# Attention score stacks of 96 and 99 rows filled with zeros to 125 and 128

## The reference

```python
mod = (silu(c) @ wmod).reshape(8, 6, 1, -1)             # shift, scale, gate, for both parts
h = layernorm(x) * (1 + ca) + sa
q, k, v = split(einsum('bnd,ed->bne', h, w_in), 3)      # 16 heads of 16 channels
scores = einsum('bhqd,bhkd->bhqk', q, k) * 16 ** -0.5
scores = where(causal, -inf, scores)                    # keys after the query
attn = softmax(scores, axis=-1)
out = einsum('bhqk,bhkd->bhqd', attn, v)
x = x + ga * (einsum('bnd,ed->bne', out, w_out) + b_out)
```

## Time and profile before

| | us |
|---|---|
| three executions | 1735.08, 1741.03, 1741.37 |
| median | 1741.03 |
| the profiled execution, own time | 1726.74 |
| its span, first to last instruction | 1725.1 |

### The profile page before, as it was taken

One profiled execution on the slowest core, in us unless ns is written; L12 is line 12 of the kernel. 1 busy time (PEld: TensorE's weight loads), 2 busy tenths in 40 slices (PEclk: granted clock), 3 DMA queues, 4 the chain that ended last, 5 costly groups with the idle time before them and its releaser, 6 DMA issues.

```text
span 1725.1 us, 33029 instructions
## 1 busy us (share of the span) xinstructions
PE 1449.8 (84%) x10024; PEld 755.3 (44%) x10024; DVE 1180.8 (68%) x2306; ACT 911.7 (53%) x1795; POOL 734.0 (43%) x876
## 2 busy tenths in 40 slices
PE   3798998788998988989898888978889789889754
PEld 2353344344543444444453444434454344544343
DVE  4668676867677776777668675787757777677342
ACT  2056655655555555565545655555545655565612
POOL 2213314454353533555344543444445453344456
PEclk9789999999998999899998999999999999999968
DMA  3211122111311122111211113111122112211100
GB/s 104 55 63 49 48 78 74 57 39 56 100 64 35 52 69 88 56 53 51 96 51 49 46 57 101 55 38 50 57 91 69 41 44 68 70 57 49 50 33 25
DMA packets 101873, 102.98 MB, mean 60 GB/s; under 512 B 21296, under 2 KB 89912, under 8 KB 101696
## 3 DMA queue, kind: packets, MB, share of 16 engines
q1 hardware_dynamic: 98176, 91.59, 16.4%
q0 software_dynamic: 2560, 8.39, 1.3%
q10 hardware_dynamic: 960, 0.79, 0.2%
HBM read 31.74 MB, written 8.94 MB: 24 GB/s over the span
## 4 chain that ended last, share of the span: by engine, by line
PE 48%; DVE 21%; issue 12%; ACT 9%; POOL 5%; SPq 2%; DMA 2%; DVEq 1%; ACTq 0%; POOLq 0%
PE row_ps L1073 9%; PE val_ps L1097 9%; PE col_ps L1043 8%; PE dense_ps L1107 7%; DVE max_a L868 7%; PE dense_ps L1109 5%; PE dense_ps L1108 5%; ACT weights L712 4%; DVE mixed L981 3%; PE row_ps L1078 2%; DVE max_b L868 2%; PE dense_ps L1126 2%; DVE xn_c L907 1%; SPq L458 1%; DVE gated L965 1%
## 5 line engine op out<-in xcount | busy, mean ns | idle before, releaser
L712 ACT ACTIVATE weights<-col_ps 128x512 f32<-128x512 f32 (+1 forms) x1216 | 620.9, 580 | 473.0 <-PE col_ps L1043 470.9
L868 DVE TENSOR_REDUCE max_a<-row_ps 128x1 f32<-128x512 f32 (+3 forms) x864 | 550.3, 663 | 238.3 <-PE row_ps L1078 155.3
L1073 PE MATMUL row_ps<-k_stack,q_stack 96*128 96x512 bf16 (+3 forms) x1536 | 469.8, 344 | 51.6 <-DVE max_a L868 33.3
L1043 PE MATMUL col_ps<-q_stack,k_stack 99*128 99x512 bf16 (+3 forms) x1536 | 400.8, 337 | 54.0 <-ACT weights L712 33.8
L594 POOL TENSOR_SCALAR_AFFINE_SELECT weights<-weights 128x512 f32<-128x512 f32 x256 | 171.0, 668 | 543.2 <-ACT weights L712 541.1
L1097 PE MATMUL val_ps<-weights,v_ones 128*32 128x512 f32 (+3 forms) x3072 | 337.0, 511 | 16.7 <-POOL weights L594 16.1
L1073 PEld LDWEIGHTS row_ps<-k_stack,q_stack 96*128 96x128 bf16 x1536 | 146.7, 100 | 354.4 <-DVE max_a L868 168.1
L868 DVE TENSOR_REDUCE max_b<-row_ps 128x1 f32<-128x384 f32 (+3 forms) x352 | 213.2, 635 | 115.0 <-PE row_ps L1078 114.7
L1043 PEld LDWEIGHTS col_ps<-q_stack,k_stack 99*128 99x128 bf16 x1536 | 133.5, 99 | 221.3 <-ACT weights L712 138.3
L1078 PE MATMUL row_ps<-causal,ident_bf 128*128 128x128 bf16 x1024 | 207.4, 227 | 0.0
L1078 PEld LDWEIGHTS row_ps<-causal,ident_bf 128*128 128x128 bf16 x1024 | 104.4, 102 | 14.8 <-issue 0.5
(11 more groups left out here) (127 smaller groups left out, 2251.6 us busy)
## 6 DMA issues: line engine op xcount, KB each, us to landing
q_stack<-q_part SPq DMA_DIRECT2D x384, 64.0 KB, 2.5
k_stack<-k_part SPq DMA_DIRECT2D x372, 64.0 KB, 2.5
xa<-in_x SPq DMA_DIRECT2D x8, 1024.0 KB, 6.6
att<-val_out SPq DMA_DIRECT2D x64, 128.0 KB
recips<-recip_rows SPq DMA_DIRECT2D x32, 256.0 KB
xq<-in_x SPq DMA_DIRECT2D x28, 256.0 KB, 3.0
out<-xq POOLq DMA_DIRECT2D x28, 256.0 KB, 2.6
q_stack<-max_rows SPq DMA_DIRECT2D x192, 4.0 KB
```

What stands on the lines that cost most here:

```text
L712: nc.scalar.activation(weights[:, t % 2, h:h + n, 0:q1 - q0], col_ps[bank][:, 0:n * (q1 - q0)].rearrange("p (h q) -> p h q", h=n), ACT.Exp ...
L868: nc.vector.reduce_max(dest, bank[:, 0:len(heads) * (k1 - k0)].rearrange("p (h k) -> p h k", h=len(heads)), AX_X).then_inc(max_done, 1)
L1043: last = nc.tensor.matmul(col_ps[bank][:, i * (q1 - q0):(i + 1) * (q1 - q0)], k_stack[s % 2][:, h, P * j:P * (j + 1)], q_stack[s % 2][:, h ...
L1073: last = nc.tensor.matmul(bank[:, n * width:(n + 1) * width], q_stack[stack][0:ROWS, h, P * i:P * (i + 1)], k_stack[stack][0:ROWS, h, k0:k ...
```

## The change

The stacks get all 128 partitions. The maximum's three rows move from 96 to 98 to 125 to 127 (`MAX_AT`). Between them and the products' rows stand zeros in `q_stack`, written once in the set-up by two further GpSimd memsets, and ones in `k_stack`, whose memset now covers 32 rows. Row-score matmuls contract rows 0 to 124 instead of 0 to 95, column-score matmuls 128 rows instead of 99. The added rows add zero to each score. The number of instructions in the loop, their moving columns, the DMAs and their sizes, and all waits stay.

```diff
@@ -43,6 +43,7 @@
 ROWS = len(Q_PARTS) * HD
 MROWS = 3
+MAX_AT = P - MROWS
 FILL = 2 * len(Q_PARTS) * 16
@@ -146,8 +147,8 @@
-        q_stack = [sb(f"q_stack{i}", [ROWS + MROWS, G, N], BF16) for i in range(2)]
-        k_stack = [sb(f"k_stack{i}", [ROWS + MROWS, G, N], BF16) for i in range(2)]
+        q_stack = [sb(f"q_stack{i}", [P, G, N], BF16) for i in range(2)]
+        k_stack = [sb(f"k_stack{i}", [P, G, N], BF16) for i in range(2)]
@@ -530,7 +531,7 @@
                         for part in range(3):
-                            sp.dma_start(q_stack[s % 2][ROWS + part:ROWS + part + 1, :, HALF:N],
+                            sp.dma_start(q_stack[s % 2][MAX_AT + part:MAX_AT + part + 1, :, HALF:N],
                                          max_rows[1][G * part:G * part + G, :]).then_inc(max_placed[1], 16)
@@ -546,7 +547,7 @@
                         for part in range(3):
-                            sp.dma_start(q_stack[(s + 1) % 2][ROWS + part:ROWS + part + 1, :, 0:HALF],
+                            sp.dma_start(q_stack[(s + 1) % 2][MAX_AT + part:MAX_AT + part + 1, :, 0:HALF],
                                          max_rows[0][G * part:G * part + G, :]).then_inc(max_placed[0], 16)
@@ -564,6 +565,8 @@
             nc.gpsimd.memset(causal[:], 0.0)
+            for stack in q_stack:
+                nc.gpsimd.memset(stack[:], 0.0)
             nc.gpsimd.memset(neg_half[:], -0.5).then_inc(consts_zero, 1)
@@ -815,7 +818,7 @@
             for i in range(2):
-                nc.vector.memset(k_stack[i][ROWS:ROWS + MROWS, :, :], 1.0)
+                nc.vector.memset(k_stack[i][ROWS:P, :, :], 1.0)
@@ -1071,8 +1074,8 @@
                     last = nc.tensor.matmul(bank[:, n * width:(n + 1) * width],
-                                            q_stack[stack][0:ROWS, h, P * i:P * (i + 1)],
-                                            k_stack[stack][0:ROWS, h, k0:k1],
+                                            q_stack[stack][0:MAX_AT, h, P * i:P * (i + 1)],
+                                            k_stack[stack][0:MAX_AT, h, k0:k1],
                                             start=(n == 0), stop=(end and not diagonal), skip_group_check=True)
```

## The result

The change makes the kernel faster: 1717.7 us median of 9 runs (1711.6 to 1731.4) against 1741.4 us of the kernel before in the same set, ratio 0.987 with a 95% interval of 0.984 to 0.991. A second set gave 1721.6 against 1736.5 us, ratio 0.989 (0.986 to 0.993). The forecast was 1722 us.

A forecast was written before the change was run, and what follows sets the result against it. It took TensorE's pace, at a mean clock of 0.947, to bound a large part of the run. Terms 0 + 0 + 0 - 16 - 3 = -19 us gave 1708 us profiled, 1722 us against the median; range 1701 to 1741 us.

The forecast's parts named there:

- Height bears on the clock: TensorE's granted clock: contracted rows count toward it; the change raises height 30% in row scores, 29% in column scores.
- Durations, nothing: Score matmuls and weight loads: cost unchanged by height, 0 us, bounds -6 to +6 us.
- The rival of loads that no longer hide: Row scores: weight loads stop overlapping running matmuls; 1756 us if a tenth of each load surfaces; chance 0.08.
- Set-up, nothing: Set-up: two added GpSimd memsets, 7.0 us taken, fit in GpSimd's 22.87 us of idle time; 0 us.
- The clock in the middle, -16 us: Middle of the run: 53 of 107 us at low clock go, at 0.3 us each.
- The start, -3 us: Near the start: an earlier clock rise saves 1.3 us before 92.5 us and 1.7 us after; bounds 0 and 5.
- The tail, nothing: Tail from 1638 us on: no score matmul is left there, so 0 us.
- The sum: Whole kernel: all terms give -19 us against the profiled 1726.74 us, so 1708 us.
- The step to the median: Whole kernel: the -19 us applied to the timed median of 1741.03 us gives 1722 us, -1.1%.
- doesn't look at height: Rival, TensorE's clock: it ignores height, so the change does nothing and time is 1741 us; chance 0.12.
- Another engine takes the gain: Rival: the clock rises but another engine bounds; 53 us give 7, the start 1, so 1733 us; chance 0.13.
- More than forecast: Rival: TensorE bounds nearly everywhere, most low spells vanish; 80 us x 0.45 + 4 = 40 us, 1701 us; chance 0.15.

The follow-up runs named there:

- half the height: The change with the maximum's rows at 112 to 114, so row scores contract 112 and column scores 115 rows; 1725.7 us, 0.995 of the kernel before.
- the set-up alone: Kernel before plus 128-row stacks and their memsets only; scores stay at 96 and 99 rows, maximum's rows at 96; 1738.1 us, ratio 0.999.
- four fillers per unit: The change plus four matmuls with unread results behind each of the drain's 20 dense units; 1711.9 us, 0.987 of the kernel before.

## Why the prediction was right

*Height bears on the clock*: shown. With the loop's instructions, columns and waits unchanged, half the height gives about half the clock, all of it 0.022, the set-up alone nothing.

*Durations, nothing*: right. Row-score loads take 99 ns (100 before), 512-column matmuls 393 and 394 ns (401 and 399), which fits the higher clock. The rival of loads that no longer hide is out.

*Set-up, nothing*: right, 6.96 us of memsets against the 7.0 taken, in idle time, and 0.999 when alone.

*The clock in the middle, -16 us*: right in kind, and its size met with luck. The first pair of profiles differs by 16.5 us there, by terms that were off in opposite directions: 68 us of low clock went instead of 53, at 0.24 us each instead of 0.3. By the second set's profile 44 us of low clock and 7.0 us of length went. The kernel with the set-up alone, in which height is as before, had 134 us low and 1553.5 us; against it the two profiles of the change are 24.6 and 15.1 us shorter. The three spells of 13.6 us ended sooner, as forecast; the longest in the middle after the change is 6.8 us. What the s = 1 rows said (0.13) and what s = 0 said (0.36) were both samples around 0.25. Groups of s = 1 take 53.4 us in the loop on average (forecast 53 to 55), those of s = 0 55.7 (forecast 54 to 55, a miss: three of the five still have a spell).

*The start, -3 us*: 2.5 us for the same work, 36.8 instead of 39.3 us from the first row-score matmul to the 61st. The first column score comes 4.7 us sooner (84.2 instead of 88.9 us), but 4.0 of these were there at the first row score, ahead of any taller matmul. The prediction took the low clock near the start to begin at 61.8 us. It was low from 45 to 58.4 us too, as the 628 ns show, where the trace has no record of it, and when it first rises differs from profile to profile.

*The tail, nothing*: wrong of the two profiled executions, +9.1 us, most of it not the change's doing. Of the eleven profiled executions without fillers in the tail all but one have 62 to 80 us low in it and 89.5 to 91.9 us of length, the set-up alone too (66 and 89.8). The kernel before's profile is the one exception, with 37 and 82.8. What the change itself does there is less clear: the seven with column scores of 128 rows have 69 to 80 us low, the four with fewer rows 37 to 66. Why is open.

*The sum*: against the profiled execution it was to be 1708 and came to 1714.8: start, middle and tail made -4.7, -16.5 and +9.1 us, and 4.0 us of the first are not the height's. The second set's profile has 1725.0. Against the median, 1722 forecast and 1717.7 measured, and 1721.6 in the second set. That the sum of -19 us lies between the medians' -23.7 and -14.9 us is in part luck. The step to the median took the profile's 183 us of low clock as typical of the kernel. The 52 timed runs of before have 0.931 on average, 239 us low, and none is over 0.944; this profile has 0.947. In part that is its late records. In part it was a good draw: beside the set-up alone, whose profile at 1738.36 us is 11.6 us longer, it has a tail 7.0 us and a middle 8.1 us shorter and a start 3.6 us longer. By the means over the timed runs 77 us of low clock went (239 to 162).

*The rivals*: "doesn't look at height" is refuted. The Trainium skill's rule that was cited for it ("TensorE: Matmul & The Clock Gate", Part 1) has the gate follow how busy TensorE has recently been. The falls that are left agree: they follow stretches with 0.36 to 1.58 us of work in 3.4. But at the same instructions the height changes the clock, which that rule does not say. "Another engine takes the gain" was right in part: 0.25 us comes back for a low microsecond instead of 0.5. "More than forecast" would have needed 0.45 each and did not come: the first median's -23.7 us are some 0.31 for each of the 77.

## What to carry to other kernels

Where TensorE's granted clock drops in stretches that are full of matmuls, look at how many rows these contract. Rows of zeros that fill up the height cost nothing per instruction here and bought 1.1 to 1.3%, while no filler matmuls for the same purpose were shown to gain more. And before a forecast goes from a profiled execution to a median, compare its mean clock with that of the timed runs and see where its records of the clock begin: low time differs from run to run, in the middle of one kernel by 25 us, and the tail's length was 9 us apart in the two profiles compared first.

## What the runs showed of the hardware

Height counts by the rows an instruction addresses, in finer steps than 32 (112 / 115 rows gave 0.944), and for zeros as well as for ones against zeros: zeros on both sides gave a clock of 0.954, zeros against ones 0.953, nothing added 0.931.

Busy time at the two levels is not the same work. In the tail of the kernel after it stayed at 1.2 GHz through 99 dense matmuls in 44.4 us:

```profile
1618.40:1662.80 44.40, 23.91 (x99) 20.87 (x97) 17.65 (x34) 8.51 (x15) 23.81 (x25) 0.50 0.09 30
```

TensorE is busy for 54% of it. In the kernel before, from 1707.0 to 1717.2 us, it was busy for 47% with the same kind of matmul, and the clock stayed up. That does not show that a low clock needs more work to rise than a high one needs to stay: at the low level a dense matmul takes longer (628 ns against 395 with the same shapes), and the low stretch holds 2.2 matmuls per us against 3.5 in the high one. So compare what goes through, and not only the busy share. With four fillers per unit the tail's low time was 27 and 20 us in the two profiles taken, without fillers 62 us or more with one exception.
